# A three-layer feature-crossing network: layer 2's sums moved next to layer 0's turn, two buffers for the relu'd values, and GpSimd's program written out without loops

## The reference

```python
def _L0_rec_ref(inputs, W0, b0, W1, b1, W2, b2):       # inputs: e, (512, 40, 32)
    h = inputs
    for i, (W, bias) in enumerate(params):               # W0 (200, 1600), W1 and W2 (200, 4000)
        x = jnp.einsum('bhd,bmd->bhmd', h, inputs).reshape(B, -1, D)
        y = jax.nn.relu(jnp.einsum('oi,bid->bod', W, x) + bias[None, :, None])
        if i != n_layers - 1:
            h, direct = jnp.split(y, 2, axis=1)          # 100 maps go on, 100 are summed
        else:
            direct = y                                   # layer 2: all 200 are summed
        outs.append(direct)
    return jnp.concatenate(outs, axis=1).sum(-1)         # 400 sums over the 32 numbers
...
    h = jnp.concatenate([z, dense_ctx], axis=1)
    h = jnp.maximum(h @ W_top1 + b_top1, 0.0)
    h = jnp.maximum(h @ W_top2 + b_top2, 0.0)
    y = h @ W_top3
```

## Time and profile before

| | before |
|---|---|
| median of three runs | 2865.26 us (2864.87 to 2867.71) |
| profiled execution, its own time | 2865.88 us |
| span in the profile | 2864.2 us |
| granted TensorE clock, mean | 0.993 of full speed |
| PE busy | 2786.2 us (97%) |
| DVE busy | 2635.1 us (92%) |
| ACT busy | 1501.6 us (52%) |
| POOL busy | 979.2 us (34%) |
| DMA, mean | 87 GB/s |

### The profile page before, as it was taken

The page is one execution under the profiler, slowest core; times in us unless marked ns, Lnnn a source line. Parts: engine busy times, 40 slices in busy tenths (PEclk is TensorE's granted clock), DMA queues, the critical chain, the costliest instruction groups (busy, mean ns, idle before and its releaser), DMA issues.

```text
span 2864.2 us, 55058 instructions
## 1 busy us (share of the span) xinstructions
PE 2786.2 (97%) x18996; PEld 2766.3 (97%) x18996; DVE 2635.1 (92%) x1939; ACT 1501.6 (52%) x1880; POOL 979.2 (34%) x950
## 2 busy tenths in 40 slices
PE   3899999999999999999999999999999999999998
PEld 3899999999999999999999999999999999999996
DVE  4899999999999999999999999999999999998993
ACT  3455555555555555555555555555555555555552
POOL 3333333333333333333333343333333344333000
PEclk8999999999999999999999999999999999999999
DMA  6433333333333333333333333433433433333321
GB/s 171 106 75 88 94 83 85 93 86 83 95 85 83 95 85 83 96 85 81 95 87 81 98 84 81 99 83 80 100 85 78 101 80 81 95 84 83 93 56 24
DMA packets 288864, 250.22 MB, mean 87 GB/s; under 512 B 33343, under 2 KB 287359, under 8 KB 288738
## 3 DMA queue, kind: packets, MB, share of 16 engines
q1 hardware_dynamic: 213192, 196.72, 24.3%
q0 software_dynamic: 66304, 45.92, 12.4%
q10 hardware_dynamic: 9344, 7.27, 0.9%
HBM read 140.74 MB, written 4.20 MB: 51 GB/s over the span
## 4 chain that ended last, share of the span: by engine, by line
PE 87%; issue 7%; DMA 2%; POOL 1%; DVE 1%; SPq 1%; ACT 1%; POOLq 0%; ACTq 0%; DVEq 0%
PE acc L755 58%; PE acc L757 27%; PE z_ps L772 1%; POOL gathered L424 1%; PE hid_ps L768 1%; DMA acc_copy<-acc_copy 1%; DVE product L676 1%; DVE tails L681 0%; DMA x_pairs<-x_rows 0%; PE acc L814 0%; POOL wait_taker L432 0%; SPq L354 0%; DMA gathered<-in_table,rows_now 0%; PE hid_ps L837 0%; ACT heads L503 0%
## 5 line engine op out<-in xcount | busy, mean ns | idle before, releaser
L755 PE MATMUL acc<-weights,heads 126*128 126x400 f32 (+1 forms) x9088 | 2710.4, 366 | 52.1 <-issue 34.4
L757 PE MATMUL acc<-weights,tails 126*128 126x200 f32 (+1 forms) x9088 | 2324.8, 256 | 0.0
L503 ACT ACTIVATE heads<-product 126x1024 fp32r<-126x1024 f32 (+2 forms) x1152 | 1202.2, 1048 | 1101.3 <-PE acc L757 535.9
L755 PEld LDWEIGHTS acc<-weights,heads 126*128 126x128 f32 (+1 forms) x9088 | 1717.7, 189 | 55.4 <-issue 42.7
L757 PEld LDWEIGHTS acc<-weights,tails 126*128 126x128 f32 (+1 forms) x9088 | 1745.2, 192 | 0.0
L681 DVE TENSOR_TENSOR tails<-product,heads 126x1024 fp32r<-126x1024 f32 (+2 forms) x1152 | 1349.5, 1204 | 3.4 <-ACT heads L503 2.2
L676 DVE TENSOR_TENSOR product<-hid_rep,x_rep 126x2048 f32<-126x2048 f32 x512 | 1172.1, 2289 | 112.7 <-PE acc L757 74.3
L432 POOL TENSOR_TENSOR wait_taker<-wait_taker 1x1 f32<-1x1 f32 x192 | 114.4, 596 | 1619.7 <-ACT acc_copy L509 1619.7
L424 POOL DMA_INDIRECT gathered<-in_table,rows_now x300 | 453.6, 1512 | 91.1 <-issue 91.1
L514 ACT ACTIVATE y_relu<-acc_copy 128x400 f32<-128x400 f32 x192 | 102.4, 533 | 196.0 <-DMA acc_copy<-acc_copy 194.1
L433 POOL DMA_DIRECT2D acc_copy<-acc_copy x192 | 191.7, 998 | 1.6 <-issue 0.3
(11 more groups left out here) (23 smaller groups left out, 126.6 us busy)
## 6 DMA issues: line engine op xcount, KB each, us to landing
x_rep<-x_rows SPq DMA_DIRECT2D x512, 120.0 KB
hid_rep<-hid SPq DMA_DIRECT2D x512, 120.0 KB
x_pairs<-x_rows SPq DMA_DIRECT2D x192, 280.0 KB
acc_copy<-acc_copy POOLq DMA_DIRECT2D x192, 200.0 KB
hid_rep<-hid SPq DMA_DIRECT2D x512, 5.0 KB
x_pairs<-x_rows SPq DMA_DIRECT2D x64, 120.0 KB
raw_weights<-in_w ACTq DMA_DIRECT2D x12, 500.0 KB, 8.5
gathered<-in_table,rows_now POOLq DMA_INDIRECT x300
```

Source lines behind the costliest of these rows:

```text
L503: act.activation(heads[0:rows, ring % HEADS_RING, 0:tiles, :], product[0:rows, ring % PRODUCT_RING, 0:tiles, :], ACT.Copy).then_inc(heads_ ...
L755: nc.tensor.matmul(acc[:, at.parity, c, 0:2 * LAYER], dims(heads[0:rows, ring % HEADS_RING, k, :], c), w, start=(q == 0 and k == 0), stop= ...
L757: last = nc.tensor.matmul(acc[:, at.parity, c, LAYER:2 * LAYER], dims(tails[0:rows, ring % PRODUCT_RING, k, :], c), w[:, 0:LAYER], start=F ...
```

## The change

It has three parts. The sums of layer 2 (`turn` of `before`), which stood on PE after two groups of layer 1, stand three groups later, directly ahead of the turn of layer 0; on ACT their copy to `z_t` moves from after group 5 of layer 1 to directly ahead of the copy of layer 0's results. `y_relu` and `y_fold` have two buffers, chosen by the slot's parity, and `relu` and `fold` wait for the turn of the slot before the previous one. POOL's program is written out: the waits stand on the DMAs themselves, `wait_taker` and `rows_now` are gone, and the two marks for SP are one-element memsets of a new tile `marker`.

```diff
-        y_relu = sb("y_relu", [128, CG, LAYER])
-        y_fold = sb("y_fold", [128, LAYER])
+        y_relu = sb("y_relu", [128, 2, CG, LAYER])
+        y_fold = sb("y_fold", [128, 2, LAYER])
...
             def add(s):
 
                 pool.wait_ge(acc_copied, s + 1)
-
-                above_zero(pool, waits_taken, s)
-                pool.tensor_tensor(wait_taker[:, 1:2], wait_taker[:, 0:1], wait_taker[:, 0:1], ALU.add).then_inc(waits_taken, 1)
                 pool.dma_start(acc_copy[:, :, 0:LAYER], acc_copy[:, :, LAYER:2 * LAYER],
                                accum_op=ALU.add).then_inc(y_summed, 16)
...
-            pool.wait_ge(first_stored[0], STORES)
             add(0)
             for b in range(1, FIRST):
                 pool.wait_ge(first_stored[b], STORES)
-            pool.tensor_tensor(wait_taker[:, 2:3], wait_taker[:, 0:1], wait_taker[:, 0:1], ALU.add).then_inc(blocks_stored, FIRST - 1)
-            pool.wait_ge(blocks_stored, FIRST - 1)
-
-            with pool.Fori(FIRST, blocks) as b:
+            pool.memset(marker[:, 0:1], 0.0).then_inc(blocks_stored, FIRST - 1)
+            pool.wait_ge(first_stored[0], STORES)
+
+            for b in range(FIRST, blocks):
                 first = 1 + (b - FIRST) * 3
-                pool.tensor_copy(rows_now[:, :], rows_all[:, bass.ds(b, 1), :].rearrange("p c k -> p (c k)")).then_inc(rows_copied, 1)
-                pool.wait_ge(rows_copied, b - (FIRST - 1))
                 add(first)
                 for k in range(FLD_DMA):
-                    gather(0, k, rows_now[:, k:k + 1], x_gathered)
+                    gather(0, k, rows_all[:, b, k:k + 1], x_gathered)
...
-                pool.tensor_tensor(wait_taker[:, 2:3], wait_taker[:, 0:1], wait_taker[:, 0:1], ALU.add).then_inc(blocks_stored, 1)
-                pool.wait_ge(blocks_stored, b)
-            done = 1 + (blocks - FIRST) * 3
-            with pool.Fori(done, total_slots) as s:
+                pool.memset(marker[:, b:b + 1], 0.0).then_inc(blocks_stored, 1)
+            for s in range(1 + (blocks - FIRST) * 3, total_slots):
                 add(s)
...
-                above_zero(act, y_turned, at.slot)
-                act.activation(y_relu[:, :, :], acc_copy[:, :, 0:LAYER], ACT.Relu).then_inc(y_relued, 1)
+                above_zero(act, y_turned, at.slot - 1)
+                act.activation(y_relu[:, at.parity, :, :], acc_copy[:, :, 0:LAYER], ACT.Relu).then_inc(y_relued, 1)
...
-                if before:
+                if before and (before[0] < 2 or not l0):
                     copy_turned(*before)
+                    before = None
...
+                if l0 and before:
+                    copy_turned(*before)
                 if l0 and first:
                     copy_turned(*l0)
...
-                above_zero(dve, y_turned, at.slot)
+                above_zero(dve, y_turned, at.slot - 1)
...
-                if l0 and before:
+                if l0 and before and before[0] < 2:
                     turn(*before)
+                    before = None
                 for q in (range(2, 5) if l0 else range(4)) if first else ():
                     accumulate(*first, q)
                 if before and not l0:
                     turn(*before)
+                if l0 and before:
+                    turn(*before)
                 if l0 and first:
                     turn(*l0)
```

More of the change, by code:

```diff
@@ L143, in cin_kernel @@
         rows_all = sb("rows_all", [128, blocks + 1, FLD_DMA], I32)
-        rows_now = sb("rows_now", [128, FLD_DMA], I32)
-        wait_taker = sb("wait_taker", [1, 3])
+        marker = sb("marker", [1, blocks])
         ident = sb("ident", [128, 128])
@@ L174, in cin_kernel @@
         rows_ready = sem("rows_ready")
-        rows_copied = sem("rows_copied")
-        taker_set = sem("taker_set")
-        waits_taken = sem("waits_taken")
         x_gathered = sem("x_gathered")
@@ L429, in add @@
                 pool.wait_ge(acc_copied, s + 1)
-                above_zero(pool, waits_taken, s)
-                pool.tensor_tensor(wait_taker[:, 1:2], wait_taker[:, 0:1], wait_taker[:, 0:1], ALU.add).then_inc(waits_taken, 1)
                 pool.dma_start(acc_copy[:, :, 0:LAYER], acc_copy[:, :, LAYER:2 * LAYER],
                                accum_op=ALU.add).then_inc(y_summed, 16)
-            pool.memset(wait_taker[:, :], 0.0).then_inc(taker_set, 1)
-            pool.wait_ge(taker_set, 1)
             pool.wait_ge(rows_ready, 1)
@@ L691, in fold @@
                 dve.wait_ge(y_relued, at.slot + 1)
-                above_zero(dve, y_turned, at.slot)
-                dve.tensor_tensor(y_fold[:, first:LAYER], y_relu[:, 0, first:LAYER], y_relu[:, 1, first:LAYER],
+                above_zero(dve, y_turned, at.slot - 1)
+                dve.tensor_tensor(y_fold[:, at.parity, first:LAYER], y_relu[:, at.parity, 0, first:LAYER],
+                                  y_relu[:, at.parity, 1, first:LAYER],
                                   ALU.add).then_inc(y_folded, 1)
@@ L767, in turn @@
                     for c in range(CG):
-                        nc.tensor.transpose(dims(hid_ps[0:HALF, layer, 0:COLS], c), y_relu[:, c, 0:HALF],
+                        nc.tensor.transpose(dims(hid_ps[0:HALF, layer, 0:COLS], c), y_relu[:, at.parity, c, 0:HALF],
                                             ident[:, :])
@@ L772, in turn @@
                     last = nc.tensor.matmul(z_ps[0:HALF, at.parity, n * BLOCK:(n + 1) * BLOCK],
-                                            y_fold[:, first:first + HALF], sum16[:, :], start=True, stop=True)
+                                            y_fold[:, at.parity, first:first + HALF], sum16[:, :], start=True, stop=True)
                 last.then_inc(y_turned, 1)
```

## The result

The changed kernel takes 2849.2 us, the median of five runs (2847.7 to 2851.34), against 2865.26 us beside it (five runs, 2860.27 to 2874.38). The ratio is 0.9943, with a 95% interval of 0.9927 to 0.9958: 16.1 us less, where 17.2 us were forecast (2848.1 us). The profiled execution takes 2849.04 us, its span is 2847.2 us and its mean granted clock 0.995.

What follows compares the result with a forecast made beforehand. PE's own stream was taken to bound the kernel, apart from a few stops beside long POOL additions. 2865.88 - 16.7 - 1.0 - 0 + 0.5 = 2848.7 us profiled, 2848.1 us for the median; range 2841 to 2858 us.

Steps and rivals of the forecast that it cites:

- The addition goes: On POOL: without the one-element addition held up beside DVE's reads, PE's stops vanish; 16.7 us gained, bounds 0 and 16.7.
- no instruction of POOL would exceed 3 us: Sign expected in the changed kernel's profile: every POOL instruction stays at or below 3 us.
- every block would take 42.84 us: Sign expected on PE: each block between 140 and 2750 us takes 42.84 us, with granted clock at 1.00.
- The ends: Near the ends, where relu waits for the DMA, the missing addition counts; 1.0 us gained, bounds -2.0 to 3.4 us.
- The sums next to the turn of layer 0: On PE, 61 passes: joining them saves nothing, cost being exposed weight loads; 0 taken, bounds 0 to 4.3 us.
- Rival A: On PE: changing between accumulation and full-precision matmuls has a price; 4.3 us more gained, 2843.8 us; chance 13%.
- ACT's copies: On ACT: `z_t` copied ahead of layer 0's `hid` makes it 0.26 us later; 0.5 us lost, at most 15.9 us.
- Rival C: Operand chain: the 0.26 us later `hid` copy reaches PE every pass; 15.9 us lost instead of 0.5, 2863.5 us; chance 11%.
- Two buffers: For relu and fold: the second buffer pays for moving the sums and brings nothing alone; 0 us.
- B: On POOL: DVE's reads hold up the DMA instead, the stops stay, only small terms remain; 2864.8 us; chance 8%.
- D: On POOL: adding DMAs held up more often than additions were, 4.2 us per stop; 2881.6 us at eight; chance 6%.

Runs made afterwards that it cites:

- e3: Changed kernel with a one-element memset, which only writes, back ahead of each adding DMA to carry the waits; 2854.69 us, ratio 0.9957 to the kernel before.
- e4: Changed kernel with the old one-element addition, which also reads SBUF, back ahead of each adding DMA; 2984.53 us, ratio 1.0395 to the kernel before.
- e9: Changed kernel with blocks 4 and 5 gathered into their own buffers right after the first adding DMA; 2848.19 us, ratio 0.9954 to the kernel before.
- e10: Changed kernel with the early gathers of e9 and layer 0's `hid` copied ahead of both `z_t`; 2847.56 us, ratio 0.9952 to the kernel before.
- c1: Changed kernel run again unaltered, as control on another chip; 2853.43 us, ratio 0.9944 to the kernel before.
- c2: Changed kernel run again unaltered, as control beside e9 and e10; 2848.09 us, ratio 0.9954 to the kernel before.
- e1: Kernel before with only GpSimd's program of the changed kernel; PE, ACT and DVE as before; 2855.12 us, ratio 0.9961 to the kernel before.
- e2: Changed kernel with the whole GpSimd program of the kernel before, so only move and buffers remain; 2873.78 us, ratio 1.0019 to the kernel before.
- e7: Changed kernel with the copy of layer 2's sums cut into eight small copies ahead of `hid`; 2856.54 us, ratio 0.9952 to the kernel before.
- e5: Changed kernel with one buffer each for `y_relu` and `y_fold`, relu and fold waiting for the slot just before; 3109.55 us, ratio 1.0870 to the kernel before.
- e6: Changed kernel with ACT copying layer 0's `hid` ahead of both `z_t` copies; 2850.82 us, ratio 0.9937 to the kernel before.

## Why the prediction was right, point by point

*The addition goes* (16.7 us). It held in kind: the stops went because the instruction that reads went, and e3 and e4 show that it is this instruction and not the waiting; that it is its read is the likeliest cause, since the memset only writes, but the two also differ in what they compute. The size was 17.6 us by the two profiles, 5.6 us of it ahead of the 4th pass, where I had worked out 5.3.

What failed are two signs: that no instruction of POOL would exceed 3 us, and that every block would take 42.84 us. I had asked whether the adding DMA would be held up and not the gathers, of which the earlier trace rows gave 300 that never exceeded 2.77 us. Two are held up, for 6.2 and 11.2 us, in the changed kernel, and at least these two in every other kernel without the addition but e9 and e10. The second costs 3.0 us there, 4.4 in c1, 3.2 in c2 and 6.5 in e1. It isn't that they read row numbers from another place, for e4's do too, and there none exceeds 3.11 us: at 120 us e4's addition is held up for 6.49 us just ahead of the gather. In the changed kernel the gather stands at that moment.

Luck has two parts in the fit. The terms that I had wrong offset each other: the spans differ by 17.6 + 2.4 - 3.0 = 17.0 us, where I had 16.7 + 1.0 - 0.5 = 17.2. And the 16.7 us came from one profile. The stops of the kernel before lie elsewhere in each execution, as its runs from 2853 to 2880 us show; by the ratios of the changed kernel, 0.9943 to 0.9954, the gain is 13 to 16 us.

*The Trainium skill* (SBUF — State Buffer, "Who interferes with whom") was weighed there. Its first half agrees with the memset of 88 to 91 ns against the addition of up to 6.57 us in the same place. Its second half, that the loser blocks until the other finishes, fits the 116 additions that take 0.46 to 0.54 us; it doesn't fit the three boundaries passed in e4.

*The ends* (1.0 us): 0.02 us. From the end of the copy to `acc_copy` to the end of the DMA's issue it is 1.45 us before, by the median of the 192, and 1.53 us after: the addition is gone, but the DMA that waits itself starts 0.3 us after its release, not 0.1, and takes 1.22 us, not 0.94. I had taken a start of 0.96 us after the release for the lower bound, from the first gather, and a value nearer to the upper one. With the addition of 2.94 us, behind which the relu waited 2.05 us, gone too, the last stretch changed by 0.02 us: nothing of that wait reached the end.

*The sums next to the turn of layer 0* (0, bounds 0 to 4.3 us): 2.4 us, in e2 as in the changed kernel. Rival A was half right: joining the two turns saves something per pass, 0.04 us and not 0.07. In the rows above it is the four loads of layer 2's sums that got shorter, 0.30 us up to the next load where it was 0.36.

*ACT's copies* (0.5 us lost): nothing in the profiles, where the waits for `x_rep` are 16 instead of 15 and no pass but the 4th is longer than 42.81 us. Rival C's condition, waits of PE for tails in many passes, didn't come even with e7's 0.42 us; 3 us in its medians stay unexplained.

*Two buffers* (0, they pay for the move): right. e5 without them costs over 250 us, of which more than half comes with the gathers that are then held up.

*Rivals B and D*: 192 adding DMAs of at most 1.34 us in the changed kernel exclude both. D's mechanism did appear in the gathers; its price per stop, 4.2 us taken, was 3.0 to 6.5.

## What to carry to other kernels

An instruction of GpSimd that reads SBUF beside a VectorE which is almost always reading two operands has no fixed price. Look at its maximum, not at its median, and count how often it is long in each version of the kernel; 3 and 23 of 64 stood at the same place here. Let the DMA or a memset carry the wait. When such an instruction goes, check the next ones on that engine that read, for they inherit its place, and check them again after every change that shifts VectorE (e5).

## What the runs showed of the hardware that was unexpected

- A one-element addition of GpSimd lasted until the end of a DVE series, 5.2 to 6.6 us and several instructions, in 35 of 192 cases of e4 and 5 of 192 of the kernel before (2.9 us at the least), and 0.46 to 0.54 us when it started late in a product. The rule that decides whether it misses a boundary stays open.
- An indirect gather is held up in the same way: 11.18 us, ending 0.96 us after DVE's series, and 11.1 to 11.2 us 55 times in e5. The adding DMAs, 192 per kernel and started by the same engine, never took more than 1.34 us in any of them.
- A DMA of GpSimd that waits itself starts 0.3 us after its release in two thirds of the cases and its issue takes 1.22 us; behind the addition it takes 0.94 us (medians).
- Eight small copies of ACT took 0.58 us together (e7), so that a further one costs about 0.06 us.
- Four weight loads of full-precision matmuls between accumulations cost 0.09 us each wherever they stand, and joining two such groups saved 0.04 us.

Open, beside that rule, are the passes that are 0.2 to 1.3 us longer in e3, c1, e6, e7 and e9, and why the changed kernel's median was 2853.43 us on the chip of the second group and 2848.09 us on that of the third. Of the 5.1 us between the two profiles 2.5 lie ahead of the 4th pass and 2.9 in the passes 4 to 63, 1.2 of these at the long gather.
